# Attention a: row maxima used with their own sign, two PSUM copies moved to ScalarE, two reductions made one

## The chip, the cores and the metric

One core of a Trainium2 chip runs the whole program. The metric is the device time of one execution in microseconds (us). The engines work side by side: TensorE (PE in the rows, PEld its weight loads), VectorE (DVE), ScalarE (ACT), GpSimd (POOL) and SyncE (SP), which issues the DMAs. They share no program order; each one goes through its own instructions in order and waits on semaphores for the others.

## What is computed

The program runs four residual blocks over x of shape 32 x 256 x 128. Only the first is touched by the change:

```python
x = x + attn_a(layernorm(x), W_qkv, b_qkv, W_out, b_out)   # 16 heads of width 8
    qkv = x @ W_qkv.T + b_qkv
    scores = einsum('bhid,bhjd->bhij', q, k) * 128 ** -0.5
    topk_scores, indices = top_k(scores, 76)                # int(256 * 0.3), per row
    masked = full(-inf); masked at the indices = topk_scores
    attn = softmax(masked, axis=-1)
    out = einsum('bhij,bhjd->bhid', attn, v)
    return out @ W_out.T + b_out
x = x + experts(layernorm(x), ...)
x = x + attn_b(layernorm(x), ...)
x = x + experts(layernorm(x), ...)
```

So attention a keeps, for each of 256 query rows of each head, the 76 largest scores, and puts a softmax over these.

## The kernel before

**Steps.** The stage of attention a goes through 64 groups of 16 tiles, two groups to a batch of x: a group is 8 heads, a tile is 128 query rows by 256 scores of one head. One step of the program (the function `step(t, b, u)`, which each engine has in its own version) works on several groups at once, each in another phase: in step t the scores of group t+1 are made and copied out, the threshold of group t is searched, the largest values of group t-1 are picked, and the softmax of groups t-2 and t-3 is put together. u = t % 4, and steps with an even u carry other side work than steps with an odd u. `schedule` unrolls the first four steps and the last eight; those between stand in a hardware loop of four steps.

**What each engine does in a step.** TensorE multiplies queries by keys into three PSUM banks (L644). VectorE copies these scores to the SBUF tile SS, 16 times 128 x 256, and each copy leaves its row maxima in `mxs` as well (`evac`, L960). ScalarE counts in three passes over the 16 tiles how many scores lie above a guessed threshold (L844, 48 instructions a step); after each pass GpSimd moves the threshold (`move`, L480 to L482). GpSimd then gives out `hi_t` and `kk` (L502, L504) with the semaphore `upper`; below `hi_t` lie the last candidates. VectorE takes from these the 16 largest per row (`largest`, L975 to L988, eight times a step, two tiles each), and `picks` chooses from the 16 values the one at the rank wanted and the one behind it: a one-hot mask `oh`, two products `pick[:, 0]` and `pick[:, 1]` (L999, L1000), and two sums over 15 values, `mid` (L1004) and `nxt` (L1005). `mid` is the threshold. GpSimd makes from SS and `mid` the tile `gone` (`outsiders`, L494), which TensorE multiplies by a steep diagonal so that all that lies under the threshold vanishes in the exponential (L678). A small check (`check_flags`) reads a flag that says whether a tile must be done again in the slow way, and gives GpSimd the semaphore `okay`.

**The row maximum.** The exponential is taken of score minus row maximum, and the subtraction is done inside the matmul: `q4x`, a copy of the transposed queries, has a row more per head. VectorE negates the maxima (`nmx`, L964, at h == 7, behind a wait for its own last copies), SyncE writes them to DRAM and reads them back as rows into `q4x` (L544 to L552), and the matching row of the keys holds ones, because ScalarE adds the column `onerow` as a bias when it copies the keys (`take_q` with m == 2, L802). SyncE waits for `nmx` before it starts these DMAs.

**The threshold's first guess.** It comes from second moments of the keys, for the batch ahead. In even steps TensorE makes keys with tokens as rows (`k_rows`, L600) into the PSUM bank M1, VectorE copies them to `ktok` (`take_k`, L914, at h == 7), and TensorE multiplies them with themselves (`moments`, L606). In odd steps TensorE makes the query rows (`q_rows`, L612, L613) into M0, VectorE copies them to `qtok` (`take_qr`, L918, at h == 3), and later multiplies them with the spread (`take_mom`, L928) and gives `var` to GpSimd (`guess`, L460).

**What sets the order.** Nothing schedules the instructions: the order on each engine is that of the code. VectorE runs `for h in range(8)`: `evac(h)`, the side work of this h, then `largest(1, h - 1)`. ScalarE runs `for h in range(9)`: at even h from 2 two exponentials (L830), then its share of the counts, then side work. A PSUM bank M0 or M1 is taken again only when the count in the semaphore `m0c` or `m1c` says that the copy of its last content is done.

Of the kernel before, what the change touches and what calls it, by code (L numbers as in the profile page):

```python
# [4 lines left out]
BATCH, T, D = 32, 256, 128  # L5
# [51 lines left out]
def build(nc, x, W_qkv, b_qkv, W_out, b_out, Wq, Wk, Wv, Wp, pos, gate_w, gate_bias,  # L57
# [7 lines left out]
    with ctx:  # L65
# [17 lines left out]
        onerow = sb("onerow", [P, 1])  # L83
# [74 lines left out]
        with nc.Block() as block:  # L158
# [65 lines left out]
            def _(dve):  # L224
# [44 lines left out]
                nc.vector.tensor_reduce(onerow[:, :], ident[:, :].rearrange("p (n w) -> p n w", w=PAD16)[:, :, HD], AX, ALU.add)  # L269
# [42 lines left out]
        def ab(name, shape, dt=f32):  # L312
# [20 lines left out]
        nmx = ab("nmx", [P, NB4, GT])  # L333
# [15 lines left out]
        mid = ab("mid", [P, NB4, GT])  # L349
# [11 lines left out]
                      "nmx copied turned spgate out pused pt pv on own aown pown slow oc gate pgate upper vput ini inid")  # L361
        nmx_rows = nc.dram_tensor("nmx_rows", (P, GT), f32, kind="Internal").ap()
# [47 lines left out]
        def m0_before(b, what):  # L410
            return before(0, b, what)
# [24 lines left out]
        with nc.Block() as block:  # L436
            @block.gpsimd
            def _(pool):
# [31 lines left out]
                def step(t, b, u):  # L470
# [14 lines left out]
                    def outsiders(lag, heads):  # L485
# [3 lines left out]
                        for h in heads:  # L489
                            wait(pool, s["pused"], 8 * (t - lag) + h - 3)  # L490
                            pool.sem_inc(s["pgate"], 1)
                            for i in range(HALVES):
                                c = 2 * h + i
                                last = pool.tensor_scalar(gone[:, h % 4, i, :], SS[:, (u - lag) % 4, c, :], mid[:, (u - lag) % 4, c:c + 1], 0.0,  # L494
                                                          ALU.subtract, ALU.min)
# [35 lines left out]
            def _(sp):  # L531
# [4 lines left out]
                def step(t, b, u):  # L536
# [3 lines left out]
                    wait(sp, s["nmx"], t + 1)  # L540
# [3 lines left out]
                    sp.dma_start(nmx_rows, nmx[:, u, :]).then_inc(s["copied"], 16)  # L544
# [4 lines left out]
                    rows = nmx_rows.rearrange("q (e g i) -> e g i q", e=2, i=HALVES)  # L549
# [237 lines left out]
            def _(act):  # L787
# [10 lines left out]
                def take_q(m, b, par, n):  # L798
                    wait(act, s["m0"], n + 1)
                    wait(act, s["copied"], COPIED * 2 * (b - 1))  # L800
                    if m == 2:
                        last = nc.scalar.activation(k4[:, par, :, :].rearrange("p c t -> p (c t)"), M0[:, :], ACT.Identity, bias=onerow[:, 0:1])  # L802
# [13 lines left out]

                take_x(0)
                for m in range(3):
                    take_q(m, 0, 0, m + 1)
                take_qn(4)  # L820
                take_v(0, 7)
# [11 lines left out]
                def step(t, b, u):  # L833
# [18 lines left out]
                    for h in range(9):  # L852
# [31 lines left out]
            def _(dve):  # L884
# [27 lines left out]
                def take_k(n):  # L912
                    wait(dve, s["m1"], n + 1)
                    V.tensor_copy(ktok[:, :, :].rearrange("p i d -> p (i d)"), M1[:, 0:T]).then_inc(s["m1c"], 1)  # L914

                def take_qr(n):
                    wait(dve, s["m0"], n + 1)
                    V.tensor_copy(qtok[:, :, :].rearrange("p i d -> p (i d)"), M0[:, 0:T]).then_inc(s["m0c"], 1)  # L918

# [16 lines left out]
                take_k(0)  # L936
                take_qr(5)
# [4 lines left out]
                def step(t, b, u):  # L942
# [7 lines left out]
                    def evac(h):  # L950
# [40 lines left out]
                    def picks():  # L991
# [15 lines left out]
                        own.need(nexts)  # L1007
# [3 lines left out]
                        positive = own.mark(V.scalar_tensor_tensor(tmp[:, :], mid[:, z2, :], 1.0e-6, nxt[:, :], ALU.is_gt, ALU.mult))  # L1011
# [905 lines left out]
```

## Time and profile before

| | before |
|---|---|
| time, median of 3 runs | 5300.36 us (5296.66 to 5301.02) |
| the profiled execution | 5302.46 us |
| its span, first to last instruction | 5300.7 us |
| mean granted TensorE clock | 0.814 |
| stage of attention a, first to last L964 | 95.2 to 2467.6 us |
| VectorE busy over the span | 4089.0 us (77%) |
| TensorE matmul busy over the span | 4709.3 us (89%) |

The profiled execution is one execution of the program; its own time is 1.8 us more than its span, which leaves out what lies before the first and behind the last instruction. In the rows "L975" is the line of the kernel, "zt<-SS,hi_t" says what is written and what is read, and a time in square brackets is idle time of the engine before the instruction with the one that ended it; "issue" is idle time for which the profile shows no such engine. In the rows of windows the numbers behind the busy times are the granted TensorE clock as a share of full speed (0.5 is 1.2 GHz, 1.0 is 2.4 GHz), the busy share of the DMA engines, and GB/s.

### The profile page before, as it was taken

What the parts mean: (1) busy time and instruction counts of PE and PEld (TensorE: products, weight loads), DVE (VectorE), ACT (ScalarE), POOL (GpSimd) and SP (SyncE); (2) the same over time, 40 slices, a digit from 0 to 9 for tenths busy, and PEclk for the clock granted to TensorE, in tenths of its full rate; (3) what the DMA queues carried; (4) which work ended last, traced back from release to release, by engine and by line L of the source; (5) the groups of instructions that cost most, each with busy time, mean ns of one, the idle gap of its engine ahead of it and who ended that gap; (6) DMA issues with size and microseconds to landing.
All of it is one profiled execution on the core that took longest, in us unless ns stands there. A gap on an engine that the chain in (4) does not pass through costs nothing. (4 is left out here: it accounts for less than half of the span.)

```text
span 5300.7 us, 121671 instructions
## 1 busy us (share of the span) xinstructions
PE 4709.3 (89%) x34686; PEld 3284.1 (62%) x34686; DVE 4089.0 (77%) x14487; ACT 3157.1 (60%) x10145; POOL 2522.7 (48%) x3026
## 2 busy tenths in 40 slices
PE   4588888889878898898899999899999998999998
PEld 3344444445444454454688888766666666888887
DVE  3899999999989999999588888655555555888886
ACT  3688888888867888887222222376777775222222
POOL 1466666666656666666544444311111111444444
PEclk6566666666656666656899999999999999999999
DMA  2000000000000000000234443200000001444444
GB/s 70 10 14 10 13 10 13 10 13 10 13 10 10 13 10 13 13 10 10 49 81 84 89 84 80 53 10 10 10 10 10 11 11 36 81 80 82 89 85 96
DMA packets 358589, 188.51 MB, mean 36 GB/s; under 512 B 190691, under 2 KB 346886, under 8 KB 358150
## 3 DMA queue, kind: packets, MB, share of 16 engines
q1 hardware_dynamic: 358150, 183.55, 17.3%
q8 instruction: 167, 2.74, 0.2%
q14 instruction: 272, 2.23, 0.1%
HBM read 147.04 MB, written 11.01 MB: 30 GB/s over the span
## 5 line engine op out<-in xcount | busy, mean ns | idle before, releaser
L844 ACT ACTIVATE junk<-SS,nt 128x256 bf16<-128x256 f32 x3072 | 1516.4, 501 | 207.1 <-POOL nt L482 156.5
L494 POOL TENSOR_SCALAR gone<-SS,mid 128x256 bf16<-128x256 f32 x1024 | 1181.9, 1171 | 759.8 <-DVEq L1038 576.5
L1205 POOL TENSOR_TENSOR f_hid<-f_g_m,f_cbs 128x256 f32<-128x256 f32 x1024 | 745.7, 728 | 849.0 <-DVE f_g_m L1450 622.5
L1305 ACT ACTIVATE f_th<-bank 128x256 f32<-128x256 f32 x1088 | 418.5, 385 | 1146.0 <-PE bank L1236 1146.0
L1235 PE MATMUL bank<-f_xTf,wgT 128*128 128x256 f32 x2176 | 692.6, 400 | 52.1 <-DVE f_g_m L1450 36.4
L1851 DVE TENSOR_REDUCE nmxb<-bank 128x2 f32<-128x512 f32 x512 | 329.2, 685 | 476.1 <-PE bank L1623 476.0
L1236 PE MATMUL bank<-f_xTf,wuT 128*128 128x256 f32 x2176 | 651.8, 381 | 0.0
L644 PE MATMUL bank<-k,q 32*128 32x256 f32 x2048 | 452.7, 574 | 220.0 <-DVE SS L960 216.6
L1267 PEld LDWEIGHTS bank<-wdT,f_hid 128*128 128x128 f32 x4096 | 601.0, 191 | 68.0 <-POOL f_hid L1205 13.2
L1267 PE MATMUL bank<-wdT,f_hid 128*128 128x128 f32 x4096 | 629.7, 276 | 11.0 <-POOL f_hid L1205 10.9
L844 ACT ACTIVATION_READ_ACCUMULATOR junk<-SS,nt 128x1 f32 x3072 | 594.0, 193 | 0.0
L975 DVE SCALAR_TENSOR_TENSOR zt<-SS,hi_t 128x256 f32<-128x256 f32 x1024 | 485.5, 514 | 89.2 <-issue 47.5
L671 PE MATMUL bank<-q4x,k4x 32*128 32x256 f32 x2048 | 535.1, 596 | 8.3 <-ACT pT L830 8.3
L1442 DVE SCALAR_TENSOR_TENSOR f_g_s<-f_th,bank 128x256 f32<-128x256 f32 x1088 | 451.3, 415 | 107.1 <-ACT f_th L1305 87.5
L1450 DVE TENSOR_TENSOR f_g_m<-f_g_s,bank 128x256 f32<-128x256 f32 x1088 | 455.9, 419 | 75.2 <-DVE f_g_s L1442 3.5
L1742 ACT ACTIVATE probb<-bank,nmxb 128x256 f32<-128x256 f32 x1024 | 441.6, 496 | 78.3 <-DVE nmxb L1851 78.3
L644 PEld LDWEIGHTS bank<-k,q 32*128 32x128 f32 x2048 | 264.2, 270 | 348.1 <-DVE SS L960 280.7
L1552 POOL TENSOR_TENSOR q<-qrow,mask_h 128x1024 f32<-128x1024 f32 x64 | 137.2, 2145 | 716.9 <-DMA qrow<-q_rows 652.9
L1236 PEld LDWEIGHTS bank<-f_xTf,wuT 128*128 128x128 f32 x2176 | 416.7, 191 | 57.4
L692 PE MATMUL bank<-pT,vaug 128*32 128x256 f32 x2048 | 425.5, 559 | 0.7 <-issue 0.6
L984 DVE MATCH_REPLACE8 zt<-L,zt 128x256 f32<-128x256 f32 x1024 | 409.0, 405 | 0.0
L830 ACT ACTIVATE pT<-bank 128x512 f32<-128x512 f32 x512 | 275.0, 588 | 220.6 <-PE bank L678 220.1
(233 smaller groups left out, 8037.1 us busy)
## 6 DMA issues: line engine op xcount, KB each, us to landing
f_cbs<-f_shares SPq DMA_DIRECT2D x512, 256.0 KB, 5.8
q4x<-q SPq DMA_DIRECT2D x64, 256.0 KB, 2.4
k4x<-k SPq DMA_DIRECT2D x64, 128.0 KB, 2.1
qrow<-q_rows SPq DMA_DIRECT2D x512, 8.0 KB
q_rows<-qTb SPq DMA_DIRECT2D x32, 128.0 KB, 1.7
out_dram<-xres SPq DMA_DIRECT2D x4, 1024.0 KB, 9.3
q4x<-nmx_rows SPq DMA_DIRECT2D x128, 4.0 KB
f_shares<-f_combT SPq DMA_DIRECT2D x64, 32.0 KB, 1.4
```

The source lines that it names most:

```text
L494: last = pool.tensor_scalar(gone[:, h % 4, i, :], SS[:, (u - lag) % 4, c, :], mid[:, (u - lag) % 4, c:c + 1], 0.0, ALU.subtract, ALU.min)
L644: last = nc.tensor.matmul(S[h % 3][:, i * T:(i + 1) * T], q4[rows(h), par, 2 * (u % 2) + h // 4, i * P:(i + 1) * P], k4[rows(h), par, u % ...
L671: nc.tensor.matmul(PT[h % 2][:, k * T:(k + 1) * T], k4x[rows(h), v, k * P:(k + 1) * P], q4x[rows(h), v, h // 4, :], start=True, stop=False)
L844: nc.scalar.activation(junk[:, c % 2, :], SS[:, uu % 4, c, :], ACT.Sign, bias=bias(c), accum_out=acc[:, k, uu % 4, c:c + 1]).then_inc(s["s ...
L975: n = own.mark(V.scalar_tensor_tensor(zt[:, i, :], SS[:, z, c, :], hi_t[:, y, c:c + 1], SS[:, z, c, :], ALU.is_le, ALU.mult))
L1205: pool.tensor_tensor(hid[:, e % NBUF, :], g_m[:, e % NBUF, :], cbs[:, par, e, :], ALU.mult).then_inc(s["hid"], 1)
L1235: nc.tensor.matmul(g[:, 0:T], wgT[:, e, :], xTf[:, par, :], start=True, stop=True)
L1236: nc.tensor.matmul(g[:, T:2 * T], wuT[:, e, :], xTf[:, par, :], start=True, stop=True).then_inc(s["gu"], 1)
L1267: last = nc.tensor.matmul(Y[par][h][:, 0:D], src[:, h * P:(h + 1) * P], wdT[:, e, :], start=(e == 0), stop=(e == NBLK - 1))
L1442: n = own.mark(V.scalar_tensor_tensor(g_s[:, e % 3, :], th[:, e % 3, :], 1.0, g[:, 0:T], ALU.add, ALU.mult))
L1450: V.tensor_tensor(g_m[:, e % NBUF if e < EB else NBUF, :], g_s[:, e % 3, :], g[:, T:2 * T], ALU.mult).then_inc(s["gm"], 1)
L1742: last = nc.scalar.activation(probb[:, u % 4, i, :], S[u % 4][:, i * T:(i + 1) * T], ACT.Exp, bias=nmx[:, u % 4, i:i + 1], scale=1.0)
```

## The change

It has three parts.

1. The maxima keep their sign. `nmx` and its instruction (L964) are gone, with the wait in front of it; SyncE waits for the copies that leave the maxima (`evac`) and writes `mxs` itself to DRAM. The keys' row gets minus one in place of one: `minusrow` in place of `onerow`, made once in the setup.
2. `take_k` and `take_qr` are ScalarE's. The copy of `ktok` goes behind the count of h == 7 in even steps, that of `qtok` behind the count of h == 2 in odd steps (where VectorE had it at h == 3), and in the prologue behind `take_qn(4)`.
3. `mid` gets room for both sums (`mid[:, z, 0]` and `mid[:, z, 1]`), and one reduction over `pick`, now 128 x 480, writes both. The comparison behind it reads them there; readers of the threshold take `mid[:, z, 0]`.

```diff
-                nc.vector.tensor_reduce(onerow[:, :], ident[:, :].rearrange("p (n w) -> p n w", w=PAD16)[:, :, HD], AX, ALU.add)
+                own.link(nc.vector.tensor_reduce(minusrow[:, :], ident[:, :].rearrange("p (n w) -> p n w", w=PAD16)[:, :, HD], AX, ALU.add))
+                nc.vector.tensor_scalar(minusrow[:, :], minusrow[:, :], -1.0, None, ALU.mult)
...
-        mid = ab("mid", [P, NB4, GT])
+        mid = ab("mid", [P, NB4, 2, GT])
...
-                    wait(sp, s["nmx"], t + 1)
+                    wait(sp, s["evac"], GT * t + GT)
...
-                    sp.dma_start(nmx_rows, nmx[:, u, :]).then_inc(s["copied"], 16)
+                    sp.dma_start(max_rows, mxs[:, u, :]).then_inc(s["copied"], 16)
...
-                        last = nc.scalar.activation(k4[:, par, :, :].rearrange("p c t -> p (c t)"), M0[:, :], ACT.Identity, bias=onerow[:, 0:1])
+                        last = nc.scalar.activation(k4[:, par, :, :].rearrange("p c t -> p (c t)"), M0[:, :], ACT.Identity, bias=minusrow[:, 0:1])
...
+                def take_k(n):
+                    wait(act, s["m1"], n + 1)
+                    nc.scalar.copy(ktok[:, :, :].rearrange("p i d -> p (i d)"), M1[:, 0:T]).then_inc(s["m1c"], 1)
+
+                def take_qr(n):
+                    wait(act, s["m0"], n + 1)
+                    nc.scalar.copy(qtok[:, :, :].rearrange("p i d -> p (i d)"), M0[:, 0:T]).then_inc(s["m0c"], 1)
...
+                            if h == 7:
+                                take_k(m1_before(bb, "ktok"))
                             if h == 8:
                                 take_qn(m0_before(bb, "qn"))
+                        if not even and front and h == 2:
+                            take_qr(m0_before(bb, "qtok"))
...
-                        if h == 7:
-                            wait(dve, s["evac"], GT * (t + 1) + GT)
-                            V.tensor_scalar(nmx[:, (u + 1) % 4, :], mxs[:, (u + 1) % 4, :], -1.0, None, ALU.mult).then_inc(s["nmx"], 1)
...
-                        mids = own.mark(V.tensor_reduce(mid[:, z2, :], pick[:, 0, :, :], AX, ALU.add))
-                        nexts = own.mark(V.tensor_reduce(nxt[:, :], pick[:, 1, :, :], AX, ALU.add))
+                        both = own.mark(V.tensor_reduce(mid[:, z2, :, :].rearrange("p a t -> p (a t)"),
+                                                        pick[:, :, :, :].rearrange("p a t j -> p (a t) j"), AX, ALU.add))
...
-                        apart = own.mark(V.tensor_tensor(nxt[:, :], nxt[:, :], mid[:, z2, :], ALU.is_lt))
+                        apart = own.mark(V.tensor_tensor(nxt[:, :], mid[:, z2, 1, :], mid[:, z2, 0, :], ALU.is_lt))
...
-                        if front and even and h == 7:
-                            take_k(m1_before(bb, "ktok"))
...
-                            if h == 3:
-                                take_qr(m0_before(bb, "qtok"))
```

On VectorE, at the end of the even steps in the loop (an instruction L960 is `evac`, L975 to L988 are `largest`), there stands before:

```order
L960 TENSOR_SCALAR SS,mxs<-bank 128x256 x2
L376 ISA
L964 TENSOR_SCALAR nmx<-mxs 128x16
L376 REGISTER_ALU
L914 COPY ktok<-bank 128x256
L975 SCALAR_TENSOR_TENSOR zt<-SS,hi_t 128x256 x2
L980 MAX L<-zt 128x8 x2
```

and now, with the lines of the changed file (L964 is `evac` there, L976 to L989 are `largest`):

```order
L964 TENSOR_SCALAR SS,mxs<-bank 128x256 x2
L976 SCALAR_TENSOR_TENSOR zt<-SS,hi_t 128x256 x2
L981 MAX L<-zt 128x8 x2
L985 MATCH_REPLACE zt<-L,zt 128x256 x2
L989 MAX L<-zt 128x8 x2
```

Two instructions with their waits are gone from between the last copy of the scores and the selection behind it; nothing else has changed places.

On ScalarE, from the copy of the keys in an even step to the first half of the odd step behind it (L844 are the counts, L830 the exponentials), there stands before:

```order
L802 ACTIVATE k<-bank,onerow 128x512
L844 ACTIVATE junk,acc<-SS,nt 128x256 x5
L830 ACTIVATE pT<-bank 128x512 x2
L844 ACTIVATE junk,acc<-SS,nt 128x256 x6
L815 ACTIVATE qnat<-bank,bnat 128x256
L844 ACTIVATE junk,acc<-SS,nt 128x256 x11
L830 ACTIVATE pT<-bank 128x512 x2
L844 ACTIVATE junk,acc<-SS,nt 128x256 x10
L830 ACTIVATE pT<-bank 128x512 x2
```

and now (L854 are the counts, L840 the exponentials):

```order
L802 ACTIVATE k<-bank,minusrow 128x512
L854 ACTIVATE junk,acc<-SS,nt 128x256 x5
L819 COPY ktok<-bank 128x256
L840 ACTIVATE pT<-bank 128x512 x2
L854 ACTIVATE junk,acc<-SS,nt 128x256 x6
L815 ACTIVATE qnat<-bank,bnat 128x256
L854 ACTIVATE junk,acc<-SS,nt 128x256 x11
L840 ACTIVATE pT<-bank 128x512 x2
L854 ACTIVATE junk,acc<-SS,nt 128x256 x5
L823 COPY qtok<-bank 128x256
L854 ACTIVATE junk,acc<-SS,nt 128x256 x5
L840 ACTIVATE pT<-bank 128x512 x2
```

The copy of `ktok` stands in front of two exponentials, and that of `qtok` between the last count of the first pass and the first count of the second.

## Rows read from the trace of the kernel before

**Rows 1.** The page, busy time of each engine over the span

```profile
PE 4709.3 (89%) x34686; PEld 3284.1 (62%) x34686; DVE 4089.0 (77%) x14487; ACT 3157.1 (60%) x10145; POOL 2522.7 (48%) x3026
```

**Rows 2.** Windows of the stage: from:to, length, busy (count) by engine, granted clock

```profile
200.00:1200.00 1000.00, 855.71 (x4181) 473.33 (x4178) 906.81 (x3526) 792.81 (x2891) 632.09 (x702) 0.63 0.07 12
```

**Rows 3.** Waits of VectorE, 200 to 2200 us: who, for whom, total us, times, longest

```profile
DVE stats L895 <- issue: 47.2, 12, 4.1
DVE zt L975 <- issue: 39.7, 28, 3.1
...
DVE SS L960 <- PE bank L644: 3.9, 8, 1.1
```

**Rows 4.** Line L964 by itself: durations in ns, first and last start

```profile
L964 DVE TENSOR_SCALAR nmx<-mxs x64: 174/174/176, 95.2 to 2467.6; 128x16 f32<-128x16 f32 x64
```

**Rows 5.** Timeline of VectorE, even step: start us, us, engine, line, operation [idle before]

```profile
1102.10 0.08 DVE L960 DVE_READ_ACCUMULATOR SS<-bank 128x1 f32 x1
1102.21 0.17 DVE L964 TENSOR_SCALAR nmx<-mxs 128x16 f32<-128x16 f32 x1
1102.31 0.42 DVE L914 COPY ktok<-bank 128x256 f32<-128x256 f32 x1
1102.65 0.87 DVE L975 SCALAR_TENSOR_TENSOR zt<-SS,hi_t 128x256 f32<-128x256 f32 x2
```

**Rows 6.** The same, end of an odd step

```profile
1137.76 0.08 DVE L960 DVE_READ_ACCUMULATOR SS<-bank 128x1 f32 x1
...
1138.11 0.29 DVE L1070 TENSOR_TENSOR xres<-xres,bank 128x128 f32 x1
```

**Rows 7.** The same, middle of an odd step

```profile
1120.34 0.08 DVE L960 DVE_READ_ACCUMULATOR SS<-bank 128x1 f32 x1
1120.34 0.42 DVE L918 COPY qtok<-bank 128x256 f32<-128x256 f32 x1
1120.67 0.87 DVE L975 SCALAR_TENSOR_TENSOR zt<-SS,hi_t 128x256 f32<-128x256 f32 x2
```

**Rows 8.** The same, next step after an odd one, and the page's row of a wider reduction

```profile
1076.25 0.39 DVE L1004 TENSOR_REDUCE mid<-pick 128x16 f32<-128x240 f32 x1
1076.56 0.39 DVE L1005 TENSOR_REDUCE nxt<-pick 128x16 f32<-128x240 f32 x1
1076.99 0.88 DVE L975 SCALAR_TENSOR_TENSOR zt<-SS,hi_t 128x256 f32<-128x256 f32 x2
...
L1851 DVE TENSOR_REDUCE nmxb<-bank 128x2 f32<-128x512 f32 x512 | 329.2, 685 | 476.1 <-PE bank L1623 476.0
```

**Rows 9.** Timeline of GpSimd over the same boundary

```profile
1053.83 4.57 POOL L494 TENSOR_SCALAR gone<-SS,mid 128x256 bf16<-128x256 f32 x4 [9.20 <-DVEq L1038]
...
1071.09 5.18 POOL L494 TENSOR_SCALAR gone<-SS,mid 128x256 bf16<-128x256 f32 x4 [0.37 <-POOL nt L463]
...
1076.59 0.20 POOL L504 TENSOR_SCALAR kk<-acc 128x16 f32<-128x16 f32 x1
```

**Rows 10.** TensorE's run before that boundary, and VectorE's first row behind it

```profile
1052.04 2.08 PE L644 MATMUL bank<-k,q 32*128 32x256 f32 x8 [0.47 <-DVE SS L960]
...
1070.38 0.42 DVE L960 TENSOR_SCALAR_CACHE_REDUCE SS<-bank 128x256 f32<-128x256 f32 x1 [0.23 <-PE bank L644]
```

**Rows 11.** TensorE and ScalarE where the two copies would go

```profile
1042.82 0.79 PE L613 MATMUL bank<-bq,ones 1*128 1x128 f32 x2
...
1044.76 0.51 ACT L844 ACTIVATE junk<-SS,nt 128x256 bf16<-128x256 f32 x1 [1.13 <-POOL nt L482]
...
1052.78 0.36 ACT L872 COPY oT<-bank 128x256 f32<-128x256 f32 x1
...
1104.24 1.06 ACT L830 ACTIVATE pT<-bank 128x512 f32<-128x512 f32 x2
...
1105.06 0.71 PE L606 MATMUL bank<-ktok 128*128 128x128 f32 x4
```

**Rows 12.** The page's group of the largest VectorE instruction

```profile
L975 DVE SCALAR_TENSOR_TENSOR zt<-SS,hi_t 128x256 f32<-128x256 f32 x1024 | 485.5, 514 | 89.2 <-issue 47.5
```

More of the change, by code:

```diff
@@ L82, in build @@
         bqs = sb("bqs", [P, 2, 2])
-        onerow = sb("onerow", [P, 1])
+        minusrow = sb("minusrow", [P, 1])
         wvT = sb("wvT", [P, D])
@@ L332, in build @@
         mxs = ab("mxs", [P, NB4, GT])
-        nmx = ab("nmx", [P, NB4, GT])
         acc = ab("acc", [P, 3, NB4, GT])
@@ L360, in build @@
         s = sems("a", "mv rstd xn m0 m0c m1 m1c var sig scores evac signs u0 u1 u2 thr failed flag okay "
-                      "nmx copied turned spgate out pused pt pv on own aown pown slow oc gate pgate upper vput ini inid")
-        nmx_rows = nc.dram_tensor("nmx_rows", (P, GT), f32, kind="Internal").ap()
+                      "copied turned spgate out pused pt pv on own aown pown slow oc gate pgate upper vput ini inid")
+        max_rows = nc.dram_tensor("max_rows", (P, GT), f32, kind="Internal").ap()
         COPIED, TURNED = 48, 32
@@ L493, in outsiders @@
                                 c = 2 * h + i
-                                last = pool.tensor_scalar(gone[:, h % 4, i, :], SS[:, (u - lag) % 4, c, :], mid[:, (u - lag) % 4, c:c + 1], 0.0,
+                                last = pool.tensor_scalar(gone[:, h % 4, i, :], SS[:, (u - lag) % 4, c, :], mid[:, (u - lag) % 4, 0, c:c + 1], 0.0,
                                                           ALU.subtract, ALU.min)
@@ L548, in step @@
                     sp.sem_inc(s["spgate"], 1)
-                    rows = nmx_rows.rearrange("q (e g i) -> e g i q", e=2, i=HALVES)
+                    rows = max_rows.rearrange("q (e g i) -> e g i q", e=2, i=HALVES)
                     for e in range(2):
@@ L820, in _ @@
                 take_qn(4)
+                take_k(0)
+                take_qr(5)
                 take_v(0, 7)
@@ L910, in normed @@
                     n.then_inc(s["xn"], 1)
[L912 to L918, printed above, removed]
                 def take_g(n):
@@ L935, in _ @@
                 normed(0)
-                take_k(0)
-                take_qr(5)
                 take_g(1)
@@ L1003, in picks @@
                         own.need(second)
-                        mids = own.mark(V.tensor_reduce(mid[:, z2, :], pick[:, 0, :, :], AX, ALU.add))
-                        nexts = own.mark(V.tensor_reduce(nxt[:, :], pick[:, 1, :, :], AX, ALU.add))
+                        both = own.mark(V.tensor_reduce(mid[:, z2, :, :].rearrange("p a t -> p (a t)"),
+                                                        pick[:, :, :, :].rearrange("p a t j -> p (a t) j"), AX, ALU.add))
                         yield
-                        own.need(nexts)
-                        apart = own.mark(V.tensor_tensor(nxt[:, :], nxt[:, :], mid[:, z2, :], ALU.is_lt))
+                        own.need(both)
+                        apart = own.mark(V.tensor_tensor(nxt[:, :], mid[:, z2, 1, :], mid[:, z2, 0, :], ALU.is_lt))
                         yield
                         own.need(apart)
-                        positive = own.mark(V.scalar_tensor_tensor(tmp[:, :], mid[:, z2, :], 1.0e-6, nxt[:, :], ALU.is_gt, ALU.mult))
+                        positive = own.mark(V.scalar_tensor_tensor(tmp[:, :], mid[:, z2, 0, :], 1.0e-6, nxt[:, :], ALU.is_gt, ALU.mult))
                         yield
@@ L1102, in redo @@
                                 slow.link(V.tensor_tensor(src, src, w, ALU.add))
-                                low = mid[:, z, bass.ds(c, 1)]
+                                low = mid[:, z, 0, bass.ds(c, 1)]
                                 slow.link(V.tensor_scalar(low, low, 0.0, -0.5 * FAR, ALU.mult, ALU.add))
```

## The prediction

> **What bounds the kernel now.** I read the busy shares first. Over the whole span TensorE leads with 4709 us against VectorE's 4089 [rows 1], which would speak against a change that relieves VectorE; but the program is four stages, and the change touches one. So I took a window inside attention a. There, of 1000 us, VectorE is busy 906.8, TensorE 855.7, ScalarE 792.8 and GpSimd 632.1 [rows 2]. Busy shares as close as these do not settle it, so I read next for whom VectorE waits. In 2000 us it waits 3.9 us for TensorE's scores; the large entries say "issue": 47.2 us in 12 pieces of up to 4.1 us, which stand where the hardware loop goes back, and 39.7 us at L975, behind the branch that looks at the flag [rows 3]. No other engine holds VectorE up. The stage runs as fast as VectorE goes through its own program, so an instruction less on it is time gained, wherever nothing else is just as late. How wide this stage is: from the first L964 to the last there are 63 steps in 2372.4 us, 37.7 us each [rows 4].
>
> **What leaves VectorE.** I price each instruction by start to start and not by its duration, since the durations overlap by some 0.08 us.
>
> - The negation and the key copy stand together at the end of even steps. The last accumulator read starts at 1102.10, L964 at 1102.21, L914 at 1102.31 and L975 at 1102.65 [rows 5]. In the odd step the copy of `qtok` starts in the same moment as the accumulator read in front of it (1120.34 both [rows 7]), so without the two instructions L975 starts at 1102.10: 0.55 us, of which 0.21 are the negation with its wait and 0.34 the copy.
> - At the end of odd steps the accumulator read starts at 1137.76 and L1070 at 1138.11 [rows 6], 0.35 us. Part of it may be register work for L1070 that would then lie open. I take 0.21, the even step's value, and keep 0.35 as the other end.
> - The copy of `qtok` is 0.33 us (1120.34 to 1120.67) [rows 7].
> - The two reductions start 0.31 us apart and the second takes 0.39, 0.70 us until the sums are there; L975 starts 0.04 behind [rows 8]. The trace has no reduction of 480. One of 512 takes 0.685, one of 240 takes 0.39 [rows 8], so 480 take about 0.65 (0.39 and 240 columns at 1.08 ns). That saves 0.05 us. Ends: nothing, and 0.31 if a wide reduction were as short as a narrow one. I stay at 0.05, since the 512 wide row is the near one.
>
> The two neighbours overlap: the second starts 0.08 us before the first ends [rows 8]. The Trainium skill, VectorE: DVE Perf Modes, section "The DRAIN you can't avoid", says that after each operation the next one does not start until the pipe is empty. By that rule the merged reduction would save a whole fixed part, 0.13 us (0.39 less 240 columns at 1.08 ns), 8 us over 62 steps where I put 3, and the sum would be 37. This trace does not agree for instructions with no wait between them, so I keep 0.05.
>
> The counts: the batch ahead exists in 31 of the 32 batches, and of 64 steps I count 62 as bound by VectorE. Even ends 31 x 0.55 = 17.1; odd ends 31 x 0.21 = 6.5; `qtok` 31 x 0.33 = 10.2; reductions 62 x 0.05 = 3.1. **Gross 36.9 us**, with the other end of the odd steps 41.2.
>
> **What is given back.** One boundary in four is tight already: from the second to the third step of a loop turn. GpSimd gets `okay`, starts `gone` at 1053.83, goes on without a real pause, and ends `kk` at 1076.79; VectorE starts the L975 that needs it at 1076.99, 0.04 us behind its own reduction [rows 8, 9]. GpSimd's chain begins with VectorE's flag in the odd step, so what VectorE saves before that flag moves both, and what it saves after it (the negation 0.21, the reductions 0.05) meets a wait. I give back 0.26 x 15 loop turns = 3.9 us. Past it `upper` comes early enough: the next boundary has the 4 us of the loop's return in it [rows 3].
>
> TensorE stands close at the same place. It starts eight score matmuls at 1052.04, after 0.47 us of waiting for VectorE, and the first copy of the next step waits 0.23 us for TensorE at 1070.38 [rows 10]. This is the same saving at the same boundary, so it is not taken off twice; where TensorE runs at the lower of its two clocks (the stage's mean is 0.63 [rows 2]) it can bite at the next one too, for which I take 1 us off in all.
>
> **What comes to ScalarE, SyncE and the setup.** A ScalarE copy of 128 x 256 out of PSUM takes 0.36 us [rows 11]; 62 of them are 22 us on an engine with 207 us free in 1000 [rows 2]. What matters is what they hold up. `qtok`: TensorE's last query row matmul ends at 1043.61, and the second pass of counts can start only at 1044.76, having waited 1.13 us for GpSimd [rows 11]. The copy fits in between. `ktok`: it stands in front of the exponentials that now start at 1104.24, and TensorE wants it at 1105.06 for L606 [rows 11], 0.8 us for a copy of 0.36. The exponentials and the counts behind it move by some 0.3 us, and the threshold of even steps is not tight. I cost both at nothing; if the cover were gone, each would cost what it is late, with the counts behind it. SyncE starts its DMAs some 0.2 us earlier and takes the same transfers; TensorE uses their rows two steps later, so nothing comes of it. The setup has one more tiny instruction, some 0.2 us. The values copied are the same, so thresholds and the tiles that must be redone should be too.
>
> **Sum:** 36.9 - 3.9 - 1.0 = 32.0 us, 0.6%. The profiled execution took 5302.5 us, which becomes 5270.5. The median of the runs is 2.1 us lower, so I forecast 5268.
>
> **Shared ports, a cost that shifts.** Four `gone` instructions take 4.57 us at 1053.83 and 5.18 us at 1071.09 [rows 9], where the products of `picks` run beside them. L975 takes 514 ns on average over 1024 [rows 12], where an undisturbed pair takes 0.87 us [rows 7], or 475 ns each with the overlap of 0.08: 39 ns x 1024 = 40 us of the stage are such meetings now. The two engines slow each other, and by how much depends on which of their instructions meet. The change moves all that remains on VectorE against GpSimd. I allow for a quarter more or less of these 40, 10 us in either direction. The Trainium skill, SBUF — State Buffer, section "Who interferes with whom", states a lock on a port pair for a VectorE instruction with two SBUF inputs beside a reading GpSimd instruction, and none for reductions. By that rule the longer `gone` rows are explained.
>
> **Rivals.**
>
> 1. *TensorE takes the place of VectorE.* It has 144 us free in 1000 [rows 2], but free time is not slack: the run from 1052.04 to 1070.38 had none behind its start [rows 10]. If both ends of a batch met TensorE, the 17.1 us of the even ends would be lost too: gain 15, time 5285. Against it speaks the 3.9 us of waiting in 2000 [rows 3]. Chance 0.12.
> 2. *The port meetings go the wrong way.* 32 - 10 = 22 us gained, 5278; the other way 42, 5258. The rows give it no sign, so each side has 0.12.
> 3. *Hardly any gain,* because the issue gaps at L975 and L1070 grow by what is taken away (the sequencer, not the datapath, would then be the limit). For it: 39.7 us of issue gaps [rows 3]. Against it: these stand behind a branch, and the removed instructions do not. Gain under 10.6 us, 5295. Chance 0.06.
> 4. *Slower: ScalarE's in-order queue.* In odd steps `take_qr` waits for TensorE's L613 with all of pass two behind it. If L613 came late, counts, threshold, `upper` and then VectorE's L975 would follow. Place: the L613 row; it ends 1.15 us before the second pass starts today [rows 11]. VectorE is reached only when the delay exceeds the time that the threshold waits in GpSimd's queue; taking the `gone` group of 5.18 us at 1071.09 [rows 9] for that, a delay of 7.5 us would cost 2.3 us a batch, 71 us in 31, and with 32 gained the kernel ends 39 slower, 5339. It decides from 6.2 us of delay (5.18 and 32 / 31). Nothing in the rows is near it. Chance 0.04.
>
> That the change doesn't do what it says is ruled out by the listings of both programs: the instructions are gone from VectorE.
>
> **Numbers.** The forecast as worked out has 0.54, port meetings 0.24, rival 1 0.12, rival 3 0.06, rival 4 0.04. Low end: all of 41.2 and 10 of better meetings, 5249. High end: rival 1 with a little, 5287. About 0.2% (10.6 us) is what a measurement can tell. Faster by more: 0.54 + 0.24 + nearly all of rival 1, 0.88. Same 0.08, slower 0.04.
>
> **What would show it.** From the end of an even step to the end of the odd one VectorE should need 0.9 us less (0.55, 0.33 and 0.05), from there to the next even end 0.3 less, and nothing less across the tight boundary. A longer gap in front of the L975 that needs `upper`, released by GpSimd, of about 0.3 us once per loop turn would confirm what is given back. Waits of VectorE for L644 beyond 20 us would speak for rival 1; a wait of ScalarE at the new `qtok` copy of more than a microsecond for rival 4. The later stages should keep their lengths. I am wrong if the stage shortens by less than 20 us or more than 45.

## The result, and the profile after

| | before | changed |
|---|---|---|
| median of 5 runs | 5301.02 us (5296.66 to 5305.3) | 5272.69 us (5271.79 to 5280.53) |
| ratio, 95% interval | | 0.9949 (0.9938 to 0.9961) |
| span of the profiled execution | 5300.7 us | 5271.0 us |
| attention a, last copy of scores of its first step to last of its last | 2372.3 us | 2342.7 us |
| first experts stage, first to last start of `f_g_s` on VectorE | 815.6 us | 815.2 us |
| attention b, first to last start of `nmxb` on VectorE | 1021.4 us | 1020.8 us |
| last experts stage, as the first | 816.5 us | 817.2 us |

The kernel is 0.5% faster. All of it comes from attention a, 29.6 of the 29.7 us of the span; the three later stages keep their lengths. The forecast was 5268, its range 5249 to 5287.

The page of the changed kernel, its busy times and its row of the largest VectorE instruction, and the window that answers to [rows 2] (busy PE, PEld, DVE, ACT, POOL, then clock, DMA share, GB/s):

```profile
PE 4705.9 (89%) x34686; PEld 3270.8 (62%) x34686; DVE 4058.1 (77%) x14296; ACT 3168.8 (60%) x10209; POOL 2528.6 (48%) x3026
...
L976 DVE SCALAR_TENSOR_TENSOR zt<-SS,hi_t 128x256 f32<-128x256 f32 x1024 | 488.6, 517 | 100.1 <-issue 56.0
```
```profile
200.00:1200.00 1000.00, 863.25 (x4246) 473.06 (x4242) 907.60 (x3490) 809.64 (x2958) 645.25 (x714) 0.63 0.07 12
```

VectorE lost 31 us of work and is as full as before inside the stage (907.6 in 1000): it still sets the pace. ScalarE has 17 us more in 1000.

VectorE's waits from 200 to 2200 us (total, number of times, longest):

```profile
DVE zt L976 <- issue: 48.3, 37, 3.1
DVE stats L909 <- issue: 48.3, 13, 4.1
DVE work L1092 <- issue: 36.3, 2, 19.3
DVE zt L976 <- DVE flags L1037: 16.0, 16, 1.0
DVE zt L976 <- DVE onrm L1027: 7.1, 13, 0.6
DVE zt L976 <- POOLq L505: 3.9, 10, 0.4
DVE SS L964 <- PE bank L644: 3.6, 5, 1.3
```

Two more of these rows of the kernel before, which [rows 3] leave out:

```profile
DVE zt L975 <- DVE flags L1036: 24.9, 25, 1.0
...
DVE zt L975 <- DVE onrm L1026: 1.9, 12, 0.2
```

One entry is new: ten waits for GpSimd's `upper` (L505), 0.4 us each, the wait that was forecast. The wait for TensorE's scores has not grown (3.6 us; before 3.9). The wait behind `onrm` has, from 1.9 to 7.1 us.

**The even end**, which answers to [rows 5]. The copy of the scores is followed by the next real work at once; the `zt` starts in the same moment as the accumulator read:

```profile
1089.69 0.08 DVE L964 DVE_READ_ACCUMULATOR SS<-bank 128x1 f32 x1
1089.69 0.87 DVE L976 SCALAR_TENSOR_TENSOR zt<-SS,hi_t 128x256 f32<-128x256 f32 x2
```

**The odd end**, which answers to [rows 6]. Here 0.35 us stood between the read and `xres`, and nothing does now, so the negation was worth all of it:

```profile
1125.36 0.07 DVE L964 DVE_READ_ACCUMULATOR SS<-bank 128x1 f32 x1
1125.36 0.47 DVE L1067 TENSOR_TENSOR xres<-xres,bank 128x128 f32 x2
```

**The tight boundary** from the second to the third step of a turn, VectorE first and GpSimd under it, which answers to [rows 8, 9]. The one reduction takes 0.65 us and is done at 1064.41; `zt` starts at 1064.80, behind `kk`, which ends at 1064.60:

```profile
1063.76 0.65 DVE L1005 TENSOR_REDUCE mid<-pick 128x32 f32<-128x480 f32 x1
1064.80 0.48 DVE L976 SCALAR_TENSOR_TENSOR zt<-SS,hi_t 128x256 f32<-128x256 f32 x1 [0.39 <-POOLq L505]
```
```profile
1059.18 4.91 POOL L494 TENSOR_SCALAR gone<-SS,mid 128x256 bf16<-128x256 f32 x4 [0.37 <-POOL nt L463]
1064.06 0.26 POOL L502 TENSOR_SCALAR hi_t<-nt 128x16 f32<-128x16 f32 x1
1064.40 0.20 POOL L504 TENSOR_SCALAR kk<-acc 128x16 f32<-128x16 f32 x1
```

**The copies on ScalarE**, one line's instructions each (min/median/max in ns, then what ScalarE waited for and who waited for the copy):

```profile
L819 ACT COPY ktok<-bank x32: 348/351/372, 74.3 to 2368.4; 128x256 f32<-128x256 f32 x32
...
  PE bank L600: 1.3, 1
...
  PEld bank L606: 2.0, 1
```
```profile
L823 ACT COPY qtok<-bank x32: 362/374/388, 76.9 to 2382.2; 128x256 f32<-128x256 f32 x32
...
  PE bank L613: 3.5, 3
```

They take 0.35 and 0.37 us. ScalarE had to wait in front of four of the 64: twice in the prologue, 1.3 and 2.2 us, and twice in the stage, 0.6 and 0.8 us, each time at `qtok`. TensorE waited for one, that of the prologue.

**The ledger.** I took from VectorE's timeline the distance from each start to the next, for the twelve loop turns from the third to the fourteenth, without steps in which a tile was redone. A turn of four steps went from 148.78 to 146.87 us, 1.91 less. Per turn:

| | us per turn |
|---|---|
| four copies, 0.34 each | 1.36 less |
| negations: even ends 0.21, odd ends 0.36, two of each | 1.14 less |
| reductions: 0.06 in three steps; in the third, 0.25 more, because of the wait for `upper` | 0.07 more |
| 16-wide comparisons (below): 0.54 more in the odd steps, 0.16 less in the third | 0.38 more |
| the two-input selections `zt<-SS,hi_t` (L975, now L976) | 0.27 more |
| gaps of VectorE's own issue | 0.07 less |
| sum | 1.85 less |

The 0.06 us that the sum lacks are spread over smaller differences.

The comparisons are the meetings with GpSimd of the prediction, at instructions that it did not name. `fine` (L1001, now L1002) and the comparison of `nxt` (L1008, now L1009) are 16 elements wide with two SBUF inputs. Groups of VectorE's instructions by line, 200 to 2200 us (busy us, mean ns), before:

```profile
L1001 DVE TENSOR_TENSOR fine<-L,hi_t 128x16 f32<-128x16 f32 x52 | 11.8, 227 | 0.0
L1008 DVE TENSOR_TENSOR nxt<-nxt,mid 128x16 f32<-128x16 f32 x52 | 8.9, 171 | 0.0
```

and after, with one such piece of VectorE's timeline and what GpSimd runs meanwhile:

```profile
L1002 DVE TENSOR_TENSOR fine<-L,hi_t 128x16 f32<-128x16 f32 x53 | 13.6, 258 | 0.0
L1009 DVE TENSOR_TENSOR nxt<-mid 128x16 f32<-128x16 f32 x53 | 12.6, 238 | 0.0
```
```profile
1097.79 0.37 DVE L1002 TENSOR_TENSOR fine<-L,hi_t 128x16 f32<-128x16 f32 x1
...
1100.32 0.36 DVE L1009 TENSOR_TENSOR nxt<-mid 128x16 f32<-128x16 f32 x1
```
```profile
1097.26 4.06 POOL L494 TENSOR_SCALAR gone<-SS,mid 128x256 bf16<-128x256 f32 x3 [0.37 <-POOL kk L504]
```

Without `gone` beside them both take 0.17 us. Beside it they take either 0.17 or 0.36 to 0.37, by where in a `gone` instruction they fall. In the kernel before, this `nxt` runs beside `gone` and is not slowed:

```profile
1112.93 0.17 DVE L1008 TENSOR_TENSOR nxt<-nxt,mid 128x16 f32<-128x16 f32 x1
```
```profile
1109.50 4.52 POOL L494 TENSOR_SCALAR gone<-SS,mid 128x256 bf16<-128x256 f32 x4 [0.37 <-PE bank L678]
```

The slowed ones start 0.4 to 0.6 us behind the start of a `gone` instruction, which then takes 1.4 to 1.6 us in place of 1.14. From 200 to 2200 us there were 15 slowed `fine` and 1 slowed `nxt` of 52 each; now there are 23 and 19 of 53. What the change did was to move them against each other. By the two groups above, the comparisons take 5 us more in these 2000, some 6 in the stage, that the change does not get. The Trainium skill, SBUF — State Buffer, section "Who interferes with whom", has a VectorE instruction with two SBUF inputs and a GpSimd instruction that reads SBUF contend for a shared port pair. The trace agrees in which instructions are slowed, and shows that a 16-wide one can lose 0.20 us, more than its own length; it also shows that some meetings of such short ones cost nothing.

### The profile page after: what moved, and what is told of

It reads as the page before. It is cut to its first block and busy times, and to the rows that moved or that the text cites. A ratio compares the mean times of both kernels' runs of the same rounds, so it can differ in the third digit from the quotient of the medians.

```text
span 5271.0 us, 121516 instructions
## 1 busy us (share of the span) xinstructions
PE 4705.9 (89%) x34686; PEld 3270.8 (62%) x34686; DVE 4058.1 (77%) x14296; ACT 3168.8 (60%) x10209; POOL 2528.6 (48%) x3026
## 5 line engine op out<-in xcount | busy, mean ns | idle before, releaser
L854 ACT ACTIVATE junk<-SS,nt 128x256 bf16<-128x256 f32 x3072 | 1516.7, 502 | 192.7 <-POOL nt L482 145.1
L494 POOL TENSOR_SCALAR gone<-SS,mid 128x256 bf16<-128x256 f32 x1024 | 1195.2, 1182 | 663.6 <-DVEq L1039 531.2
L854 ACT ACTIVATION_READ_ACCUMULATOR junk<-SS,nt 128x1 f32 x3072 | 597.7, 195 | 0.0
L644 PE MATMUL bank<-k,q 32*128 32x256 f32 x2048 | 428.8, 553 | 165.6 <-DVE SS L964 160.0
L976 DVE SCALAR_TENSOR_TENSOR zt<-SS,hi_t 128x256 f32<-128x256 f32 x1024 | 488.6, 517 | 100.1 <-issue 56.0
L644 PEld LDWEIGHTS bank<-k,q 32*128 32x128 f32 x2048 | 249.6, 261 | 296.9 <-DVE SS L964 225.9
L964 DVE TENSOR_SCALAR_CACHE_REDUCE SS<-bank 128x256 f32<-128x256 f32 x1024 | 384.4, 412 | 32.2 <-PE bank L644 28.4
```

The costliest lines, as they stand in the source:

```text
L644: last = nc.tensor.matmul(S[h % 3][:, i * T:(i + 1) * T], q4[rows(h), par, 2 * (u % 2) + h // 4, i * P:(i + 1) * P], k4[rows(h), par, u % ...
L854: nc.scalar.activation(junk[:, c % 2, :], SS[:, uu % 4, c, :], ACT.Sign, bias=bias(c), accum_out=acc[:, k, uu % 4, c:c + 1]).then_inc(s["s ...
L976: n = own.mark(V.scalar_tensor_tensor(zt[:, i, :], SS[:, z, c, :], hi_t[:, y, c:c + 1], SS[:, z, c, :], ALU.is_le, ALU.mult))
```

## The experiments

### Each part alone

Three kernels are the one before with one part of the change. The first has part 1 (nothing negated, minus ones in the keys' row), the second part 2 (both copies on ScalarE), the third part 3 (one reduction). The fourth is the changed kernel with two reductions again:

```diff
-                        both = own.mark(V.tensor_reduce(mid[:, z2, :, :].rearrange("p a t -> p (a t)"),
-                                                        pick[:, :, :, :].rearrange("p a t j -> p (a t) j"), AX, ALU.add))
+                        mids = own.mark(V.tensor_reduce(mid[:, z2, :], pick[:, 0, :, :], AX, ALU.add))
+                        nexts = own.mark(V.tensor_reduce(nxt[:, :], pick[:, 1, :, :], AX, ALU.add))
```

> Only the maxima part. My theory (VectorE's own program is the length of the stage, each instruction priced start to start): even ends save 0.21 us, odd ends 0.36 plus a register gap of up to 0.3 in front of the addition to xres; across the tight boundary (second to third step of a loop turn) the saving is met by the wait for upper. Gain 12 to 20 us of span. Rival (TensorE takes over at the step ends): under 8 us.

> Only the two copies on ScalarE. My theory: 31 x (0.34 + 0.34) = 21 us gained, ScalarE waits for neither copy by more than a few tenths. Rival (TensorE takes over at the ends of even steps): the key copy's 10.5 us are lost, about 11 us gained. Rival (ScalarE's queue): no gain or slower.

> Only the merged reduction. My theory: 0.06 us saved in three steps of four, nothing or a small loss in the step behind the tight boundary, where upper ends last: 2 to 3 us gained, not to be told from no change. Rival (each instruction carries its whole fixed cost, 0.13): 8 us gained. Rival (the merged form meets GpSimd worse): slower by 5 us or more.

> The change without its third part. If the merged reduction is what lengthens the step behind the tight boundary, this one is as fast as the whole change or faster by up to 4 us; if the 0.13 us longer starts behind the fine and nxt comparisons in odd steps come from the merged form, they are gone here (8 us in all); if they come from how VectorE and GpSimd meet, they stay.

| kernel | median, us | ratio to before (95%) | attention a | a turn of four steps |
|---|---|---|---|---|
| before | 5300.18 | | 2372.3 | 148.78 |
| part 1 alone | 5279.53 | 0.9966 (0.9952 to 0.998) | 2345.8 | 146.90 |
| part 2 alone | 5272.8 | 0.9947 (0.9931 to 0.9964) | 2342.7 | 146.86 |
| part 3 alone | 5289.45 | 0.998 (0.9971 to 0.999) | 2357.4 | 147.86 |
| parts 1 and 2 | 5414.87 | 1.0214 (1.0197 to 1.0231) | 2343.1 | 146.96 |
| the change | 5272.69 | 0.9949 (0.9938 to 0.9961) | 2342.7 | 146.87 |

By the medians the parts alone gained 20.7, 27.4 and 10.7 us, where 12 to 20, 21 and 2 to 3 were expected: all three more. Two things are not as expected. First, the parts don't add up: 1.88, 1.92 and 0.92 us per turn alone, 4.72 together, and the change gives 1.91. Part 2 alone gives all that the change gives. Its work is 1.36 us per turn, that of part 1 is 1.14, that of part 3 is 0.24 (four times 0.06). So part 3 gets four times what it removes. It comes near the 8 us of its rival, but not by the rival's way: the reductions themselves give 0.18 us per turn. The rest is gaps of issue. The same waits of VectorE as above, kernel by kernel; part 1 alone:

```profile
DVE stats L895 <- issue: 46.5, 13, 4.0
...
DVE zt L972 <- DVE flags L1033: 36.6, 37, 1.0
DVE zt L972 <- issue: 23.7, 16, 3.1
```

part 2 alone:

```profile
DVE stats L909 <- issue: 43.3, 13, 3.6
...
DVE zt L979 <- DVE flags L1040: 35.6, 36, 1.0
DVE zt L979 <- issue: 24.7, 17, 3.1
```

part 3 alone:

```profile
DVE stats L895 <- issue: 41.6, 12, 3.8
...
DVE zt L975 <- issue: 30.9, 23, 3.1
DVE zt L975 <- DVE flags L1036: 29.7, 30, 1.0
```

The two rows of `zt`, mostly the gap behind the branch on the flag, hold 64.6 us before and 64.3 in the change, but 60.3, 60.3 and 60.6 in the three parts: in one step of each turn the gap is 1.0 us in place of 1.3. The loop's return (`stats`) takes 3.9 us before (47.2 / 12), and 3.6, 3.3 and 3.5 in the parts. In the ledger all such gaps together are 7.90 us per turn before, 7.02, 6.76 and 6.91 with one part, and 7.83 with all three. The instructions behind these gaps are the same in all kernels; what differs is where they stand in VectorE's program, and the work around them. Each single part thus got some 1 us per turn, about 15 us, on top of its work and less what it lost elsewhere, and the whole change got next to nothing of it. It has the shorter gap of the third step too, but 0.39 us more behind `onrm` in the first step, 0.3 more behind the flag in the fourth, and a longer return than the parts.

Second, parts 1 and 2 without part 3 are 115 us slower than the kernel before, and attention a is not the cause: it is as short as in the change. The last experts stage, which no edit touches, takes 961.7 us in place of 817. The next kernels look at both. (What the fourth kernel was built for: its wait for `upper` is 7.0 us in ten pieces, where the change has 3.9, so the merged reduction does not cause it. Its comparisons are 0.27 us longer than before in the second step, as in the change, and as short as before in the fourth. Two reductions in place of one don't cure them; what decides is where they meet `gone`.)

### The boundary that waits for GpSimd, and the place of the code

In the first kernel GpSimd gives out `hi_t`, `kk` and `upper` for the third step of a turn one step earlier, ahead of its last `gone` group, so that VectorE does not wait for them:

```diff
-                    if runs(t, 1):
+                    def bounds(t, u):
...
+                    if runs(t, 1) and u != 2:
+                        bounds(t, u)
...
+                    if u == 1 and runs(t + 1, 1):
+                        bounds(t + 1, u + 1)
```

The second is the change with eight one-column memsets in VectorE's prologue of attention a; with the instruction that closes them, VectorE's program is nine instructions longer from there on. The third is the change again.

```diff
+                for _ in range(8):
+                    own.link(V.memset(work[:, 0:1], 0.0))
```

> The change, and in GpSimd's program the two bounds hi_t and kk of the third step of a turn stand in front of the last four gone instructions of the second. If the wait at L976 that is left once per turn (0.39 us, 15 turns, 6 us in all) is for GpSimd's late bounds, it goes away: 4 to 6 us faster than the change. If something else ends last there (TensorE's scores, VectorE's own reduction), 0 to 2 us. The gone instructions come 0.6 us later; should TensorE's subtraction need them, TensorE's waits for gone grow.

> The change, with eight tiny linked memsets on VectorE ahead of the stage's loop, some 1.3 us, so that all of VectorE's later code lies elsewhere in memory. Theory (the issue gaps at the flag's branch, at the normalisation and at the addition to xres depend on where the code lies): these gaps change places by 0.2 to 0.4 us per turn, as they did between before and after, and the sum moves by up to 6 us either way. Rival (they depend on what waits for what): the gaps stay where they are, and the span grows by 1 to 2 us.

> The change itself once more, on the chip of the two runs beside it: a gain of 25 to 30 us over the kernel before.

The change again gave 5271.16 us (ratio 0.9943, 0.9926 to 0.9959), attention a 2344.4. With the 2341.1 of a kernel below, whose code is the same up to the end of attention b, the stage's length repeats within some 3 us.

The early bounds gave 5273.54 us (0.9949, 0.9932 to 0.9966), no gain. The wait for `upper` is gone: reductions and wait of the third step go from 0.99 to 0.68 us per turn. But the fourth step is 0.33 longer, in front of its first copy of scores, where VectorE now waits for TensorE: from 200 to 2200 us it waits for scores 17 times, 8.7 us, in place of 5 times and 3.6. What it no longer waits for GpSimd in the third step it waits for TensorE at the start of the fourth.

The eight memsets gave 5396.16 us (1.0184, 1.0167 to 1.0201). Attention a is 4.5 us shorter (2338.2). Two of its gaps are as in the single parts again, behind `onrm` and behind the flag in the fourth step, though nothing but the place of the code has changed around them:

```profile
DVE zt L978 <- DVE flags L1039: 35.6, 36, 1.0
DVE zt L978 <- issue: 25.0, 17, 3.1
...
DVE zt L978 <- DVE onrm L1029: 2.0, 13, 0.2
```

The last experts stage is 944.9 us, 128 longer. This was not expected at all, and it looks like what happened without part 3: a stage that the edit does not touch. The next kernels test whether the place of the code does it.

### The place alone

Four kernels with the memsets: nine of them at the end of attention b's program on VectorE (so only the last experts stage moves, to the place that the eight gave it); eight in attention a and eighteen more at the end of attention b (which moves the last stage past the bad place); eight in the kernel before; and eight and eighteen together with the early bounds.

> The change, with nine tiny memsets on VectorE behind the last use of attention b, so that only the code of the last experts stage lies elsewhere, at the instruction number that it has in the run with eight memsets ahead of the first loop. If the place of VectorE's code in memory is what made that run's last stage 128 us longer, this one's last stage is longer by 110 to 150 us with an unchanged stage of attention a. If it was anything that the first stage left behind, the last stage keeps its 817 us.

> The change with eight memsets ahead of the first loop and eighteen behind attention b: the code of attention a lies where it lay in the shifted run (whose stage was 4 to 6 us shorter than the change's), that of the last stage where it lies in the runs of single parts. By the theory of places the last stage is back at 816 to 818 us and the whole at 5266 to 5270, faster than the change by 2 to 6 us. Otherwise it stays near 5395.

> The kernel before with eight memsets ahead of the first loop, no work taken away. If the kernel before has 0.9 us per loop turn of fetch gaps that its place in memory gives it (at the addition to xres, behind the flag in the third step, at the loop's return), its attention a shortens by about 14 us. If these gaps belong to its order of work, it stays at 2372. The last stage is open: fast or some 130 us longer.

> The last but one with GpSimd's bounds given out early in the second step: if the wait that is left at the tight boundary counts where TensorE is not late, 3 to 5 us less than without; if TensorE's scores take its place, the same.

| kernel | number of the first instruction of the last experts loop, counted in VectorE's listing | last experts stage, us | attention a, us | median, us (ratio, 95%) |
|---|---|---|---|---|
| the change | 3286 | 817.2 | 2342.7 | 5272.69 (0.9949) |
| nine, late | 3295 | 942.2 | 2341.1 | 5401.85 (1.0189, 1.0172 to 1.0206) |
| eight, early | 3295 | 944.9 | 2338.2 | 5396.16 (1.0184, 1.0167 to 1.0201) |
| parts 1 and 2 | 3298 | 961.7 | 2343.1 | 5414.87 (1.0214, 1.0197 to 1.0231) |
| part 1 alone | 3312 | 817.6 | 2345.8 | 5279.53 (0.9966) |
| part 2 alone | 3313 | 815.8 | 2342.7 | 5272.8 (0.9947) |
| eight, and eighteen late | 3313 | 816.2 | 2336.1 | 5269.2 (0.9941, 0.9925 to 0.9958) |
| the same, early bounds | 3313 | 816.0 | 2324.9 | 5263.67 (0.9926, 0.991 to 0.9943) |
| part 3 alone | 3315 | 815.6 | 2357.4 | 5289.45 (0.998) |
| before | 3327 | 816.5 | 2372.3 | 5301.02 |
| before, eight | 3336 | 817.4 | 2371.1 | 5302.3 (0.9999, 0.999 to 1.0009) |

Each median stands beside the kernel before of its own round; the four of this section ran beside a before of 5302.92. Nine idle instructions, executed once, cost 125 us: the change and the kernel with the nine differ in nothing else. Where the time goes is seen in VectorE's waits from 4440 to 5200 us. In the kernel with the nine late ones:

```profile
DVE f_g_s L1439 <- issue: 108.2, 24, 8.2
...
DVE f_g_s L1439 <- ACT f_th L1302: 25.9, 65, 2.0
```

In the change, as in each of the other kernels whose last stage takes 817 us, VectorE has no row of issue in this stretch (the three with a long last stage have 84.2 to 108.2 us at this line):

```profile
DVE f_g_s L1439 <- ACT f_th L1302: 34.9, 88, 0.5
```

The first long gap in VectorE's timeline of the kernel with the nine:

```profile
4523.71 0.42 DVE L1439 SCALAR_TENSOR_TENSOR f_g_s<-f_th,bank 128x256 f32<-128x256 f32 x1 [7.41 <-issue]
```

It stands where the hardware loop goes back. VectorE, for whose `f_g_s` and `f_g_m` the other engines wait there, is without an instruction for 7 us, and again for 1.7 some 3 us later. The stage has 14 such returns; at some 9 us each they make the 125.

What goes on in these gaps can be seen in the DMA queues. The profile has two queues of the kind "instruction" (packets, MB, share). Over the whole run, the change:

```profile
q14 instruction: 259, 2.12, 0.1%
```

and the kernel with the nine:

```profile
q14 instruction: 329, 2.70, 0.2%
```

Those are 70 more, five for each of the 14 returns. From 4440 to 5200 us the three kernels with a long last stage move 64 or 65 packets of 8 KB on this queue, the ten others 6 to 8. At the first long gap of the kernel with the nine (4516.30 to 4523.71), two start at 4520.0 and 4520.7 and take 0.7 and 1.0 us; the next starts at 4525.2, just before the gap of 1.71 us. So at a bad place of the loop instructions are fetched anew at each return, and elsewhere they are not. The profile doesn't name the engine that a packet is for, but these two kernels differ on VectorE alone. The packets fill only part of a gap; what the rest of it is, no run shows. Which places are bad stays open: starts at 3295 and 3298 are, and 3286 and 3312 to 3336 are not.

**For attention a** the place matters less, and not in the way I thought. Its loop moves instructions on this queue in every kernel, 199 to 212 packets of 8 KB from 200 to 2200 us. The eight early memsets shorten it by 4.5 and 6.6 us (2338.2, 2336.1) when they stand in the change, not much more than the 3 us by which it varies. In the kernel before they do nothing: the gaps shrink by 0.78 us per turn, as the theory has it, but the third step becomes 0.70 longer, 0.37 of it a wait in front of its first copies, which the profile puts down to TensorE in eight of twelve turns, and a turn is 0.25 shorter only. The expected gain of some 14 us did not come. Of what VectorE's issue gave back, TensorE took about half; the rest of the longer third step has no cause that the runs show.

**Both together** are the best kernel. With the early bounds but without the shift: no gain. With the shift but without the early bounds: 3.5 us by the medians, within what a measurement tells. With both: 5263.67 us (5262.0 to 5264.97), 39 less than before, where the change gains 28, and 5.5 less than the shift alone in the same round (5268.17 to 5278.03; 3 to 5 were expected). A turn is 145.57 us against 146.46: 0.23 of it is the wait for `upper`, 0.35 less waiting for TensorE in front of first copies, 0.14 the loop's return. So the wait for `upper`, which the early bounds were built for, is about a quarter of it. The 11 us by which attention a is shorter are not all kept: behind its last copy of scores VectorE waits longer for TensorE, and the span is 6 us shorter. VectorE's waits from 200 to 2200 us in it have no row of `upper`:

```profile
DVE stats L914 <- issue: 48.4, 13, 4.0
DVE zt L983 <- DVE flags L1044: 37.6, 38, 1.0
DVE work L1099 <- issue: 36.3, 2, 19.3
DVE zt L983 <- issue: 23.8, 16, 3.1
DVE SS L971 <- PE bank L649: 5.2, 11, 0.8
```

## Why the prediction was right, and where it was not

The sum held: 32.0 us less was forecast and 29.7 came, all in the stage named. But errors of several terms cancelled, which is luck, and the steps did not hold equally.

- **VectorE sets the pace: right.** The stage got shorter by what left VectorE, less what is named below. VectorE is as full as before, and part 2 alone, which only takes copies off VectorE, shortens the stage by 29.6 us, of which the copies are some 20 and shorter gaps of issue the rest.
- **The copies, 0.34 and 0.33 us: right,** and hidden on ScalarE. `qtok` waited three times for L613; the longest wait, 2.2 us, is in the prologue, the two in the stage are under the microsecond that was set as a sign. Rival 4 (ScalarE's in-order queue, from 6.2 us of delay) did not occur.
- **The negation: mis-sized.** I took 0.21 us at odd ends and kept 0.35 as the other end; 0.36 left. Per turn that is 0.30 more than taken, some 4.7 us. The even ends' 0.21 was right.
- **The reductions: right.** 480 wide take 0.64 to 0.65 us; 0.06 is saved per step where I put 0.05. The 0.13 that a full wait between neighbours would have given did not come. The section of the Trainium skill that the prediction cites (VectorE: DVE Perf Modes, "The DRAIN you can't avoid") has the exception itself: a next operation that is not held starts earlier. The two reductions did, by 0.08 us [rows 8].
- **The tight boundary: right in place, releaser and about in size.** 0.26 us was forecast; the waits are up to 0.39, and the third step's reductions and wait cost 0.25 more than before.
- **TensorE: nearly as late, at no price.** Its matmuls for the first copy of the second and fourth step ended 2.8 and 2.2 us ahead of that copy before (medians), and 0.46 now in both, the shortest distance that any of these traces has: nothing is left in hand. The loss of 17.1 us that rival 1 is made of did not come: VectorE waits 3.6 us in 2000. But the early bounds alone gained nothing, because VectorE then waited for TensorE at the next first copy.
- **Port meetings: the right mechanism at instructions that I had not looked at.** I priced them at L975, whose mean went from 514 to 517 ns: 3 us (4 by the ledger). Some 6 us were lost at the 16-wide comparisons. Together they are nearly the whole allowance of 10.
- **The distribution over the steps: wrong.** I had 0.9 us less in odd steps, 0.3 in the step behind the loop's return and nothing across the tight boundary. Measured from the last copy of scores of one step to that of the next: 0.41 (step ending behind the loop's return), 0.66 (second), 0.40 (third, across the tight boundary), 0.45 (fourth). The odd steps lost 0.27 each to the meetings. The third gained at the gap behind the flag (1.30 to 1.00 us), for which the fourth gave 0.28 back, and the first at the loop's return and at `xres`.
- **"Issue gaps" as fixed: the step that failed as an assumption.** I let them stand and weighed only whether they would swallow the gain. They differ by up to 1.1 us per turn between these kernels, as much as part 1 removes, and by 0.78 through eight idle instructions alone; only because they stayed in sum (7.90 to 7.83) did the total come out. That later stages keep their lengths came true for the change, but not as a matter of course: nine instructions more made the kernel 1.9% slower than before.

Open is the rule of the place, in both loops; with it, why the three parts' gains in the gaps vanish together; and part of why the third step of the kernel before becomes longer when the eight memsets are there.

## What to carry to other kernels

Price an edit on the engine that sets the pace by start to start, at each place where it stands: the same instruction was worth 0.21 us at one end and 0.36 at the other. Before a part of a change is given the credit, or the blame, look at the stages that it does not touch and at the bounding engine's gaps of issue at loop returns, since there a shift of the program by a few instructions can outweigh the edit; a kernel that only adds idle instructions tells the two apart, and the packets of the instruction queues show where it happens. Where a second engine is just in time, relieving the first shows nothing until the second has moved.

## What the runs showed of the hardware

- VectorE's return to the head of a hardware loop depends on where the loop lies in its program: no gap of issue in the last experts stage at most places, 7.41 us and then 1.7 at a start of 3295. Over the stage that is 125 us for nine added instructions, and 145 us at 3298.
- The fetch shows in the profile as packets of 8 KB on q14, kind "instruction": 65 in 760 us with the last experts loop at 3295, 6 with it at 3286.
- In attention a eight idle instructions alone change the return from 3.9 to 3.7 us (in the kernel before), one gap behind the branch on the flag from 1.3 to 1.0, and the gap behind `onrm` from 0.6 to 0.2 (in the change).
- A 16-wide VectorE comparison with two SBUF inputs takes 0.17 or 0.37 us beside GpSimd's `gone`, by where in it the comparison falls; the `gone` that slows it takes 1.4 to 1.6 us in place of 1.14.
